# Mamba's chunk-end states: two sets of sums on four 32-column groups in place of a chain of six steps

## The chip, the cores and the metric

The kernel runs on one core of a Trainium2 chip. The metric is the device time of one execution in microseconds (us). TensorE is PE in the profile (its weight loads are PEld), VectorE is DVE, ScalarE is ACT, GpSimd is POOL, and SP is the engine that issues most DMAs.

## The reference

A decoder block: Mamba with two layers, cross-attention, and a mixture of experts, each behind a layer norm. Only Mamba matters here. Its recurrence, cut to the core:

```python
def scan_fn(carry, inp):
    h, v = carry
    dA_t, mi_t, C_t = inp
    v = BETA * v + mi_t          # BETA = 0.6
    h = dA_t * h + v
    y_t = jnp.einsum('ben,bn->be', h, C_t)
    return ((h, v), y_t)
```

`mi_t` is the outer product of a row of 512 channels (`delta * x`) and a row of 16 numbers (`B`). There are 4 sequences of 512 tokens and 2 layers. The inner recurrence `v` has a constant factor, so it is a convolution with powers of 0.6, and the kernel makes it with matmuls.

## The kernel before

Mamba is done in 8 **stages**, k = 0 to 7 (layer k // 4, sequence k % 4). A stage has 64 **pieces** i = 64k to 64k + 63; a piece is one of 16 states for 128 of the 512 channels, over all 512 tokens. For each pair of pieces TensorE makes `v` in two PSUM banks (`L631`, 24 matmuls), VectorE scans `h` over it (`L783`), GpSimd multiplies by `C` (`L987`), and TensorE adds the result of the piece 7 places back into an output bank by transposing it (`L610`, `pe_add_state`). ScalarE makes the decays `dA` (`L923`), issued 3 pieces ahead.

The matmul of `v` works on 6 chunks of 43 or 42 tokens for each half (256 tokens) of the sequence. `uT` holds a chunk in 64 partitions, rows 0 to 63 for the first half and 64 to 127 for the second. The first 16 rows of each block hold the state `v` at the end of the chunk before; the rest are the tokens. So before a stage can start, its chunk-end states must be known and put into these 16 rows. `bend` holds the weights that turn a block into its end state. That is what changes:

- `mid` (`L561`) adds up all 6 chunks of the first half, 12 matmuls of 64x256 (two groups of 64 columns), and gives the end state of the first half; ScalarE copies it (`act_carry`, `L802`).
- Then 5 steps, `c` and `ch` together (`L569`): the end of chunk c from the block of chunk c, in both halves at once, 4 matmuls of 64x256 on the four 64x64 tiles, then 4 copies of 16x256, and only then the next step.

Stage 0 has this chain in the open (`plan_first`). The front of a stage k + 1 is done during stage k: each engine's list `steps` says after which piece it does which part (`plan_front`); on TensorE the parts in `TILED` stand between the matmuls of `v` of a pair and the additions. There `mid` is at piece 50, and the five steps are at pieces 52, 54, 56, 58 and 60. I call the time from `mid` to the first `v` of the next stage the **end stretch**. `L550` (`u`) is the transposition of the chunks ahead of it.

Six PSUM banks are handed out by `banks_for`, in the order of `rows`: a single part takes the bank that was taken longest ago, a pair of pieces two neighbouring banks. `pe_open` waits until the bank's last user is through; for a pair's bank that is both scans of the pair.

Of the kernel before, what the change touches and what calls it, by code (L numbers as in the profile page):

```python
# [15 lines left out]
P = 128  # L16
BETA = 0.6
# [8 lines left out]
MID = 64  # L26
TILED = ("mid", "c", "ch")
# [48 lines left out]
def build(nc, d, out):  # L76
# [14 lines left out]
    with ExitStack() as ctx:  # L91
# [5 lines left out]
        def sb(c, name, shape, dt=F32):  # L97
            return c.enter_context(nc.sbuf_tensor(name, shape, dt))
# [102 lines left out]
        with ExitStack() as mc:  # L201
# [10 lines left out]
            ends = sb(mc, "ends", [P, NCH, 2])  # L212
# [15 lines left out]
            bend = lay(NCH * P).rearrange("p (c n) -> p c n", c=NCH)  # L228
# [47 lines left out]
            def plan_first():  # L276
# [23 lines left out]
                put("dve", "bcol")  # L300
                for m in range(ET):
                    put("pe", "d", m)
                    s += m % 2
                    put("act", "d", m)
# [25 lines left out]
                put("pe", "mid", 0)  # L330
                s += 1
                put("act", "mid", 0)
                for c in range(NCH - 1):
                    s += 1
                    for part in ("c", "ch"):
                        put("pe", part, c)
                    s += 1
                    for part in ("c", "ch"):
                        put("act", part, c)

            def plan_front(k, at, start):
# [16 lines left out]
                put(23, "dve", "bcol")  # L358
                for m in range(ET):
# [17 lines left out]
                put(50, "pe", "mid", 0)  # L377
                put(50, "act", "mid", 0)
                for c in range(NCH - 1):
                    for part in ("c", "ch"):  # L380
                        put(52 + 2 * c, "pe", part, c)
                        put(52 + 2 * c, "act", part, c)
# [89 lines left out]
            TAKER = {"xn": "dve", "p": "dve", "z": "act", "xp": "act", "dbcT": "dve", "d": "act", "u": "act", "mid": "act", "c": "act", "ch": "act", "bt": "dve", "bo": "dve", "ak": "dve", "aq": "dve", "ax": "act"}  # L472
# [27 lines left out]
            def pe_side(k, what, j=0):  # L500
# [54 lines left out]
                elif what == "mid":  # L555
                    bk = pe_open(k, "mid", 0)
                    pe.wait_ge(bend_done, k + 1)
                    pe.wait_ge(bank_act, emptied_by("act", k, "u", NCH - 1))
# [4 lines left out]
                elif what == "c":  # L563
                    sides = [pe_open(k, part, j) for part in ("c", "ch")]
                    pe.wait_ge(bank_act, emptied_by("act", k, "ch", j - 1) if j else emptied_by("act", k, "mid", 0))
                    for e0 in range(2):
                        for half in range(2):
                            r0 = half * KT
                            i = pe.matmul(sides[half][e0 * MT:(e0 + 1) * MT, e0 * HS:(e0 + 1) * HS], bend[r0:r0 + KT, j, 0:MT],  # L569
                                          uT[par][r0:r0 + KT, j, e0 * HS:(e0 + 1) * HS], start=True, stop=True, tile_position=(r0, e0 * MT))  # L570
                            if e0:
                                i.then_inc(bank_full, 1)
                    return
                elif what == "ch":
# [90 lines left out]
            def dve_side(k, what, j=0):  # L665
# [16 lines left out]
                elif what == "bcol":  # L682
                    dve.wait_ge(bank_full, filled(k, "dbcT", 0))
                    dve.wait_ge(ld_scan, 64)
                    if k >= 2:
# [4 lines left out]
                    dve.wait_ge(bank_dve, emptied_by("dve", k, "dbcT", 0))  # L690
                    dve.tensor_tensor(bend.rearrange("p c (g n) -> p c g n", g=2)[:, :, :, 0:NSTATE],
                                      bcol[:, par].unsqueeze(2).to_broadcast([P, NCH, 2, NSTATE]),
                                      ends[:].unsqueeze(3).to_broadcast([P, NCH, 2, NSTATE]), ALU.mult).then_inc(bend_done, 1)
# [105 lines left out]
            def act_carry(dst, bk):  # L799
                for e0 in range(2):  # L800
                    cols = slice(e0 * HS, (e0 + 1) * HS)
                    i = act.copy(dst[0:NSTATE, cols], bk[e0 * MT:e0 * MT + NSTATE, cols])  # L802
                i.then_inc(bank_act, 1)

            def act_side(k, what, j=0):
# [11 lines left out]
                elif what == "p":  # L817
                    bk = bank(k, "p", j)
                    act.wait_ge(bank_full, filled(k, "p", j))
                    if k == 0 and j == 0:  # L820
                        act.wait_ge(zeroed, 5)
                        act.wait_ge(ld_conv, 32)
# [64 lines left out]
                elif what in ("c", "ch"):  # L887
                    act.wait_ge(bank_full, filled(k, "ch", j))
                    act_carry(uT[par][KT * (what == "ch"):, j + 1, :], bank(k, what, j))
                elif what == "mid":  # L890
                    act.wait_ge(bank_full, filled(k, "mid", 0))
                    act_carry(uT[par][KT:, 0, :], bank(k, "mid", 0))
# [72 lines left out]
            def pool_mamba():  # L965
# [4 lines left out]
                pool.memset(bend, 0.0).then_inc(zeroed, 1)  # L970
                pool.wait_ge(zeroed, 5)
# [1030 lines left out]
def shape_constants():  # L2002
# [6 lines left out]
    ends = np.zeros((2, KT, len(CHUNKS), 2), np.float64)  # L2009
    for c, (t0, width) in enumerate(CHUNKS):  # L2010
        for half in range(2):
            ends[half, :, c, 0] = toep[half, :, width - 1]
        ends[0, NSTATE:NSTATE + width, c, 1] = BETA ** (CHUNKS[-1][0] + CHUNKS[-1][1] - 1 - t0 - np.arange(width))
    toep, ends = toep.reshape(P, QC), ends.reshape(P, len(CHUNKS), 2)
# [85 lines left out]
```

## Time and profile before

| | us |
|---|---|
| median of 3 runs (1557.35 to 1559.39) | 1558.73 |
| the profiled execution's own time | 1560.36 |
| its span | 1558.9 |
| Mamba until the first `v` of stage 0 | 78.4 |
| `mid` of stage 1 to `mid` of stage 7 (171.40 to 854.21), per stage | 113.8 |
| TensorE busy, share of the span | 88% |

All times are read on one execution's trace, from its first instruction. `x24` in a row is a count of instructions; an f32 matmul is recorded as two. "Idle before" in brackets names what the engine waited for.

### The profile page before, as it was taken

How to read it: one execution, taken by the hardware profiler on the slowest of the kernel's cores; microseconds unless marked ns; L12 is line 12 of the kernel's file. 1: busy time of each engine (PE TensorE's matmuls, PEld its weight loads, DVE VectorE, ACT ScalarE, POOL GpSimd, SP SyncE). 2: the span in 40 equal slices, each digit the busy share in tenths (PEclk: the TensorE clock that was granted, in tenths of full speed). 3: DMA queues.
4: the chain of work that ended last, by engine and by line, in shares of the span. 5: the costliest groups of instructions: out<-in, count | busy, mean ns of one | idle time of the engine just before them, and what ended most of it. 6: DMA issues, size and time to landing. Idle time of an engine off the chain costs nothing.

```text
span 1558.9 us, 46788 instructions
## 1 busy us (share of the span) xinstructions
PE 1372.9 (88%) x20442; PEld 975.9 (63%) x20442; DVE 1066.0 (68%) x1347; ACT 908.8 (58%) x1365; POOL 921.2 (59%) x802
## 2 busy tenths in 40 slices
PE   4679799999899899899899886878989887999997
PEld 2357577777677677667677775533444343499996
DVE  4189898798689688788788786577676771422223
ACT  3658567777767667767666765116555655434440
POOL 1159888989979969969969986530303000035541
PEclk8689999999999999999999998969999999999999
DMA  4102212222212212221221344370414100612225
GB/s 134 49 28 85 83 65 75 85 83 96 84 71 84 84 57 84 84 72 69 87 81 70 138 128 125 76 149 1 84 39 85 24 1 15 264 47 69 68 66 179
DMA packets 41497, 127.26 MB, mean 82 GB/s; under 512 B 8784, under 2 KB 21584, under 8 KB 32848
## 3 DMA queue, kind: packets, MB, share of 16 engines
q1 hardware_dynamic: 34736, 108.27, 21.4%
q0 software_dynamic: 6048, 14.95, 3.6%
q8 instruction: 163, 2.67, 0.7%
q10 hardware_dynamic: 512, 1.05, 0.4%
q14 instruction: 38, 0.31, 0.1%
HBM read 97.90 MB, written 9.57 MB: 69 GB/s over the span
## 4 chain that ended last, share of the span: by engine, by line
PE 59%; DVE 20%; issue 10%; ACT 4%; POOL 4%; DMA 2%; DVEq 0%; SPq 0%; ACTq 0%; POOLq 0%
PE psum L631 12%; DVE hst L783 9%; PE psum L610 8%; PE psum L1710 4%; PE psum L1722 4%; PE psum L1298 4%; PE psum L515 3%; POOL hst L987 3%; PE psum L601 3%; DVE overlay L679 2%; PE psum L1280 2%; DVE w_early L783 2%; PE psum L1652 2%; PE psum L1264 2%; DVE nmax L1419 2%
## 5 line engine op out<-in xcount | busy, mean ns | idle before, releaser
L987 POOL TENSOR_TENSOR hst<-hst,cb 128x512 f32<-128x512 f32 x399 | 513.5, 1306 | 125.7 <-DVE hst L783 110.3
L783 DVE TENSOR_TENSOR_SCAN hst<-dA,psum 128x512 f32<-128x512 f32 x399 | 467.1, 1204 | 140.7 <-PE psum L631 140.4
L610 PE MATMUL psum<-ident,hst 128*128 128x128 f32 x1596 | 236.5, 282 | 15.6 <-POOL hst L987 12.7
L610 PEld LDWEIGHTS psum<-ident,hst 128*128 128x128 f32 x1596 | 174.2, 141 | 66.3 <-issue 25.4
L923 ACT ACTIVATE dA<-delta,alog 128x512 f32<-128x512 f32 x256 | 177.0, 718 | 63.1 <-DVE hst L783 43.9
L923 ACT ACTIVATE dA<-xres,alog 128x512 f32<-128x512 f32 x256 | 176.1, 718 | 47.8 <-DVE hst L783 35.6
L1419 DVE TENSOR_REDUCE nmax<-psum 128x2 f32<-128x1024 f32 x128 | 154.6, 1220 | 55.3 <-PE psum L1264 54.8
L1348 ACT ACTIVATE pT<-psum 128x1024 f32<-128x1024 f32 x128 | 128.0, 1024 | 102.9 <-PE psum L1284 79.3
L631 PE MATMUL psum<-filt,c_early 64*64 64x86 f32 (+1 forms) x6144 | 147.2, 241 | 32.8 <-DVE hst L783 23.6
L631 PEld LDWEIGHTS psum<-filt,c_early 64*64 64x64 f32 x6144 | 126.6, 136 | 68.8 <-issue 39.9
L631 PE MATMUL psum<-filt,uT 64*64 64x86 f32 (+1 forms) x6144 | 144.8, 238 | 23.8 <-DVE hst L783 14.6
L631 PEld LDWEIGHTS psum<-filt,uT 64*64 64x64 f32 x6144 | 123.8, 133 | 57.2 <-issue 38.0
L987 POOL TENSOR_TENSOR w_early<-w_early,cb 128x512 f32<-128x512 f32 x113 | 144.5, 1290 | 24.5 <-DVE w_early L783 24.2
L783 DVE TENSOR_TENSOR_SCAN w_early<-dA,psum 128x512 f32<-128x512 f32 x113 | 133.8, 1204 | 30.2 <-PE psum L631 29.9
L1955 POOL DMA_INDIRECT overlay<-x_hat,origin x39 | 37.8, 970 | 186.6 <-DVE c_early L1901 175.1
L515 PE MATMUL psum<-overlay,w_early 128*128 128x512 f32 x256 | 124.4, 614 | 1.9 <-DVE hst L783 1.1
L1961 POOL DMA_INDIRECT y_choice<-yb,goal x39 | 38.5, 986 | 70.0 <-DVE yb L1915 70.0
L1800 ACT ACTIVATE ht<-psum 128x512 f32<-128x512 f32 x39 | 23.3, 597 | 93.9 <-PE psum L1710 93.9
L1710 PEld LDWEIGHTS psum<-xt,xn 128*128 128x128 f32 x624 | 75.6, 192 | 2.8 <-DVE xt L1907 0.9
L1710 PE MATMUL psum<-xt,xn 128*128 128x128 f32 x624 | 76.1, 275 | 0.7 <-DVE xt L1907 0.7
L679 DVE SCALAR_TENSOR_TENSOR overlay<-psum,w_cv,overlay 128x509 f32<-128x509 f32 (+2 forms) x96 | 71.1, 742 | 7.6 <-ACT overlay L823 5.3
L1722 PE MATMUL psum<-w_down,ht 128*128 x312 | 73.7, 380 | 0.0
(236 smaller groups left out, 2130.5 us busy)
## 6 DMA issues: line engine op xcount, KB each, us to landing
cb<-c_rows SPq DMA_DIRECT2D x64, 1024.0 KB, 4.7
qk_first<-w_early SPq DMA_DIRECT2D x64, 64.0 KB, 2.4
qk<-part SPq DMA_DIRECT2D x64, 64.0 KB, 2.7
w_up<-up_dram SPq DMA_DIRECT2D x8, 512.0 KB, 7.3
w_down<-down_dram SPq DMA_DIRECT2D x8, 512.0 KB, 12.9
w_up<-y_choice SPq DMA_DIRECT2D x8, 512.0 KB, 6.9
qk<-part POOLq DMA_DIRECT2D x48, 64.0 KB, 5.2
qk_first<-part SPq DMA_DIRECT2D x40, 64.0 KB, 2.4
```

The source lines that it names most:

```text
L515: i = pe.matmul(bk, w_in[:, kt, m8 * P:(m8 + 1) * P], xnT[:, kt, :], start=kt == 0, stop=kt == KD - 1)
L610: m = pe.matmul(psum[:, Y0 + et % EP, t * P:(t + 1) * P], hst(i)[:, t * P:(t + 1) * P], ident[:], start=n == 0 and t == 0, stop=n == NSTAT ...
L631: m = pe.matmul(halves_at[half][e0:e0 + MT, :, t0:t0 + width], uT[k % 2][r0:r0 + KT, c, et * P + e0:et * P + e0 + MT], filt[r0:r0 + KT, f ...
L679: i = dve.scalar_tensor_tensor(out=dst, in0=bk[:, 0:S - late], scalar=w_cv[:, l, j, tap:tap + 1], in1=dst, op0=ALU.mult, op1=ALU.add)
L783: dve.tensor_tensor_scan(hst(i), a, v, 0.0, ALU.mult, ALU.add).then_inc(scan_done, 1)
L923: act.activation(dA[:, a % NDA, :], delta[k % 2][:, et, :], ACT.Exp, scale=alog[:, k // B, et, n:n + 1]).then_inc(decay_done, 1)
L987: pool.tensor_tensor(h, h, cb[:, q % 2, state_of(i)[1] % GN, :], ALU.mult).then_inc(g_done, 1)
L1298: m = pe.matmul(psum[i * HROW:(i + 1) * HROW, PV, :], vt[:, cp, kv, c0:c0 + HROW], pT[:, (m0 + i // 2) % NPT, i % 2, :], start=kv == 0, st ...
L1348: act.activation(pT[:, m % NPT], pair(u, "score", s), ACT.Exp, scale=HDIM ** -0.5).then_inc(pair_act, 1)
L1419: dve.tensor_reduce(nmax[:, u % 2, t, 2 * j:2 * j + 2], pair(u, "max", r), AX.X, ALU.max, negate=True).then_inc(pair_dve, 1)
L1710: m = pe.matmul(psum[:, U0 + j % NUB, ft * P:(ft + 1) * P], wu[:, j % NWU, kt * F + ft * P:kt * F + (ft + 1) * P], xt[:, j % NXT, kt, :], ...
L1722: m = pe.matmul(out_bank(j)[:, 0:D], ht[:, j % NHT, ft, :], w_down[:, bass.ds(at + ft * D, D)], start=ft == 0, stop=ft == FT - 1)
```

## The change

The end states of a half are no longer a chain. `bend` becomes 6 x 6 blocks of 16 columns: for each end e and chunk c the powers of 0.6 that carry chunk c to end e. The ends of a half are six sums, over 1 to 6 chunks. `lo` makes the six ends of the first half, 21 matmuls of 16 x 512 with rows 0 to 63; each end has one of four 32-column groups in one of two banks (`LO_AT`), and the matmuls are issued in turns over the groups, 6 turns in all. ScalarE copies the six ends (16x512 each). `hi` makes five ends of the second half from rows 64 to 127, 15 matmuls in 5 turns (`HI_AT`), and 5 copies follow. `hi` needs the last end of `lo` and its copies. `bend` is now made by GpSimd (128x576) and no longer by VectorE (128x192, `L691`), in `plan_front` at piece 26.

```diff
-                put("pe", "mid", 0)
-                s += 1
-                put("act", "mid", 0)
-                for c in range(NCH - 1):
+                for part in ("lo", "hi"):
+                    for n in range(2):
+                        put("pe", part, n)
...
-                put(50, "pe", "mid", 0)
-                put(50, "act", "mid", 0)
-                for c in range(NCH - 1):
-                    for part in ("c", "ch"):
-                        put(52 + 2 * c, "pe", part, c)
-                        put(52 + 2 * c, "act", part, c)
+                for part, s in (("lo", 50), ("hi", 56)):
+                    for n in range(2):
+                        put(s, "pe", part, n)
+                        put(s + n, "act", part, n)
...
+LO_AT = ((5, 4, 3, 2), (None, None, 0, 1))
+HI_AT = ((4, 3, 2, 1), (None, None, 0, None))
...
-                    for c in range(NCH):
-                        for e0 in range(2):
-                            i = pe.matmul(bk[e0 * MT:(e0 + 1) * MT, e0 * HS:(e0 + 1) * HS], bend[0:KT, c, MID:MID + MT], uT[par][0:KT, c, e0 * HS:(e0 + 1) * HS],
-                                          start=c == 0, stop=c == NCH - 1, tile_position=(0, e0 * MT))
...
+                    sides = [pe_open(k, what, n) for n in range(2)]
+                    if what == "lo":
+                        pe.wait_ge(bend_done, k + 1)
+                        pe.wait_ge(bank_act, emptied_by("act", k, "u", NCH - 1))
+                    else:
+                        pe.wait_ge(bank_act, emptied_by("act", k, "lo", 1))
+                    at, r0 = (LO_AT, 0) if what == "lo" else (HI_AT, KT)
+                    queues = [[(n, at[n][g], c) for n in range(2) if at[n][g] is not None for c in range(at[n][g] + 1)] for g in range(4)]
+                    for turn in range(NCH):
+                        for g in range(4):
+                            if turn < len(queues[g]):
+                                n, end, c = queues[g][turn]
+                                i = pe.matmul(sides[n][g * BC:g * BC + NSTATE, :], bend[r0:r0 + KT, end, c, :], uT[par][r0:r0 + KT, c, :],
+                                              start=c == 0, stop=c == end, tile_position=(r0, g * BC))
+                    i.then_inc(bank_full, 2)
...
+                elif what in ("lo", "hi"):
+                    act.wait_ge(bank_full, filled(k, what, 1))
+                    for g, end in enumerate((LO_AT if what == "lo" else HI_AT)[j]):
+                        if end is not None:
+                            r0, c = (0 if what == "lo" else KT, end + 1) if end < NCH - 1 else (KT, 0)
+                            i = act.copy(uT[par][r0:r0 + NSTATE, c, :], bank(k, what, j)[g * BC:g * BC + NSTATE, :])
+                    i.then_inc(bank_act, 1)
...
+                if what == "bend":
+                    pool.wait_ge(bank_dve, emptied_by("dve", k, "dbcT", 0))
...
+                    pool.tensor_tensor(bend, bcol[:, par].unsqueeze(1).to_broadcast([P, NCH, NCH, NSTATE]),
+                                       ends[:].unsqueeze(3).to_broadcast([P, NCH, NCH, NSTATE]), ALU.mult).then_inc(bend_done, 1)
```

TensorE's order in the end stretch of stages 1 to 7 (here during stage 3) was, from the pair at piece 50 on (`L631` is `v`, `L610` the additions, `L561` is `mid`, `L569` is `c` with `ch`):

```order
L561 MATMUL psum<-c_early,overlay 64x256 x12
L610 MATMUL psum<-ident,hst 128x128 x8
L631 MATMUL psum<-filt,uT 64x2x43 x16
L631 MATMUL psum<-filt,uT 64x2x42 x8
L569 MATMUL psum<-c_early,overlay 64x256 x4
L610 MATMUL psum<-ident,hst 128x128 x8
```

The last four rows come five times. In the changed kernel the lines are numbered `L568` (`lo`, `hi`), `L627` (`v`) and `L606` (additions), and at the same place stands:

```order
L568 MATMUL psum<-c_early,overlay 16x512 x21
L606 MATMUL psum<-ident,hst 128x128 x8
L627 MATMUL psum<-filt,uT 64x2x43 x16
L627 MATMUL psum<-filt,uT 64x2x42 x8
L606 MATMUL psum<-ident,hst 128x128 x8
L627 MATMUL psum<-filt,uT 64x2x43 x16
L627 MATMUL psum<-filt,uT 64x2x42 x8
L606 MATMUL psum<-ident,hst 128x128 x8
L627 MATMUL psum<-filt,uT 64x2x43 x16
L627 MATMUL psum<-filt,uT 64x2x42 x8
L568 MATMUL psum<-c_early,overlay 16x512 x15
```

Six small insertions have become two large ones, at pieces 50 and 56; pieces 58, 60 and 62 follow with nothing between. The banks follow: before, pieces 54, 56, 58, 60 and 62 (from stage 2's pieces on) all get the two banks that the pair just ahead of them left; after, every pair from 52 to 62 gets banks of a user at least three entries of `rows` back.

ScalarE's order there was (`L923` decays, `L802` copies of ends), the last two rows five times:

```order
L923 ACTIVATE dA<-xres,alog 128x512
L802 COPY uT<-psum 16x256 x2
L923 ACTIVATE dA<-xres,alog 128x512 x2
L802 COPY uT<-psum 16x256 x4
L923 ACTIVATE dA<-xres,alog 128x512 x2
```

and is now (`L910` decays, `L878` copies):

```order
L910 ACTIVATE dA<-xres,alog 128x512
L878 COPY uT<-psum 16x512 x4
L910 ACTIVATE dA<-xres,alog 128x512
L878 COPY uT<-psum 16x512 x2
L910 ACTIVATE dA<-xres,alog 128x512 x5
L878 COPY uT<-psum 16x512 x4
L910 ACTIVATE dA<-xres,alog 128x512
L878 COPY uT<-psum 16x512
```

There are 11 copies in four places instead of 22 in six.

## Rows read from the trace of the kernel before

**Rows 1.** The page, busy time and share of the span, instructions.

```profile
PE 1372.9 (88%) x20442; PEld 975.9 (63%) x20442; DVE 1066.0 (68%) x1347; ACT 908.8 (58%) x1365; POOL 921.2 (59%) x802
```

**Rows 2.** Waits of VectorE in the end stretches 171:202, 290:310, 627:652.

```profile
DVE hst L783 <- PE psum L631: 4.5, 2, 2.3
...
DVE hst L783 <- PE psum L631: 2.9, 5, 1.4
DVE w_early L783 <- PE psum L631: 2.8, 2, 2.3
...
DVE hst L783 <- PE psum L631: 8.8, 6, 2.3
DVE w_early L783 <- PE psum L631: 1.4, 1, 1.4
```

**Rows 3.** Timeline of stage 0's chain: start, us, engine, line.

```profile
58.09 5.21 PE L561 MATMUL psum<-c_early,overlay 64*64 64x256 f32 x24 [1.30 <-ACT c_early L885]
65.43 1.50 ACT L802 COPY c_early<-psum 16x256 f32<-16x256 f32 x4 [1.36 <-PE psum L569]
...
78.40 3.69 PE L631 MATMUL psum<-filt,c_early 64*64 64x86 f32 x96 [1.63 <-ACT c_early L802]
```

**Rows 4.** Windows (PE, PEld, DVE, ACT, POOL busy; granted clock; DMA share; GB/s).

```profile
59.00:63.30 4.30, 4.30 (x21) 2.42 (x17) 0.00 (x0) 0.00 (x0) 0.00 (x0) 0.50 0.00 0
...
78.90:82.10 3.20, 3.20 (x92) 2.94 (x84) 1.57 (x2) 3.19 (x5) 0.20 (x1) 0.50 0.00 0
83.00:89.00 6.00, 4.01 (x151) 3.62 (x152) 5.86 (x15) 5.69 (x8) 4.00 (x5) 1.00 0.01 3
```

**Rows 5.** Timeline, attention: matmuls on four 32-column groups.

```profile
1104.48 1.07 PE L1298 MATMUL psum<-pT,vt 128*32 128x512 f32 x8
...
1107.76 1.92 PE L1298 MATMUL psum<-pT,vt 128*32 128x512 f32 x16
```

**Rows 6.** Timeline, ScalarE: four copies of 512 columns from PSUM.

```profile
47.15 2.03 ACT L827 COPY xres<-psum 128x512 f32<-128x512 f32 x4
```

**Rows 7.** Timeline of stage 6's end stretch, during stage 5.

```profile
627.09 2.76 PE L561 MATMUL psum<-uT,overlay 64*64 64x256 f32 x24
...
629.78 1.09 PE L610 MATMUL psum<-ident,hst 128*128 128x128 f32 x8
...
649.40 1.12 PE L631 MATMUL psum<-filt,c_early 64*64 64x86 f32 x48 [1.14 <-DVE hst L783]
...
650.63 4.55 DVE L783 TENSOR_TENSOR_SCAN hst<-dA,psum 128x512 f32<-128x512 f32 x4 [1.38 <-PE psum L631]
```

**Rows 8.** Timeline around stage 2's end stretch, during stage 1.

```profile
290.21 2.76 PE L561 MATMUL psum<-c_early,overlay 64*64 64x256 f32 x24
...
309.25 6.77 DVE L783 TENSOR_TENSOR_SCAN hst<-dA,psum 128x512 f32<-128x512 f32 x6 [0.20 <-PE psum L631]
```

**Rows 9.** Timeline, TensorE: `v` of stages 1 and 5, `mid` of stage 3.

```profile
201.75 0.46 PE L631 MATMUL psum<-filt,uT 64*64 64x86 f32 x12
...
398.92 0.38 PE L561 MATMUL psum<-uT,overlay 64*64 64x256 f32 x1
...
537.50 1.12 PE L631 MATMUL psum<-filt,c_early 64*64 64x86 f32 x48
...
539.57 1.12 PE L631 MATMUL psum<-filt,c_early 64*64 64x86 f32 x48
```

**Rows 10.** Timeline of stage 1's end stretch, during stage 0.

```profile
171.40 2.81 PE L561 MATMUL psum<-uT,overlay 64*64 64x256 f32 x24 [0.43 <-DVE hst L783]
...
174.32 4.08 DVE L756 TENSOR_SCALAR stat<-stat 128x8 f32<-128x8 f32 x1
```

**Rows 11.** By line: `bend` on VectorE, and GpSimd's filters; timeline of GpSimd.

```profile
L691 DVE TENSOR_TENSOR overlay<-bcol,ends x8: 357/1441/1446, 36.8 to 810.5; 128x192 f32<-128x192 f32 x8
...
L959 POOL TENSOR_TENSOR filt<-toep,bcol x64: 1049/1054/1507, 51.0 to 877.8; 128x516 f32<-128x516 f32 x64
...
586.38 2.70 POOL L987 TENSOR_TENSOR hst<-hst,cb 128x512 f32<-128x512 f32 x2 [1.67 <-DVE hst L783]
```

More of the change, by code:

```diff
@@ L25 @@
 MT = 64
-MID = 64
-TILED = ("mid", "c", "ch")
+LO_AT = ((5, 4, 3, 2), (None, None, 0, 1))
+HI_AT = ((4, 3, 2, 1), (None, None, 0, None))
+TILED = ("lo", "hi")
 EP, NFILT = 2, 9
@@ L211, in build @@
             toep = sb(mc, "toep", [P, QC])
-            ends = sb(mc, "ends", [P, NCH, 2])
+            ends = sb(mc, "ends", [P, NCH, NCH])
             keep = sb(mc, "keep", [P, 1])
@@ L227, in build @@
             bcol = sb(mc, "bcol", [P, 2, NCH, NSTATE])
-            bend = lay(NCH * P).rearrange("p (c n) -> p c n", c=NCH)
+            bend = lay(NCH * P)[:, 0:NCH * NCH * NSTATE].rearrange("p (e c n) -> p e c n", e=NCH, c=NCH)
             filt = sb(mc, "filt", [P, NFILT, NCH, 2, QC])
@@ L300, in plan_first @@
                 put("dve", "bcol")
+                put("pool", "bend")
                 for m in range(ET):
@@ L358, in plan_front @@
                 put(23, "dve", "bcol")
+                put(26, "pool", "bend")
                 for m in range(ET):
@@ L376, in plan_front @@
                     put(45 + c // 2 * 2, "act", "u", c)
-                put(50, "pe", "mid", 0)
-                put(50, "act", "mid", 0)
-                for c in range(NCH - 1):
-                    for part in ("c", "ch"):
-                        put(52 + 2 * c, "pe", part, c)
-                        put(52 + 2 * c, "act", part, c)
+                for part, s in (("lo", 50), ("hi", 56)):
+                    for n in range(2):
+                        put(s, "pe", part, n)
+                        put(s + n, "act", part, n)
             def plan_back(k, at, s):
@@ L554, in pe_side @@
                     return
[L555 to L558, printed above, removed]
-                    for c in range(NCH):
-                        for e0 in range(2):
-                            i = pe.matmul(bk[e0 * MT:(e0 + 1) * MT, e0 * HS:(e0 + 1) * HS], bend[0:KT, c, MID:MID + MT], uT[par][0:KT, c, e0 * HS:(e0 + 1) * HS],
-                                          start=c == 0, stop=c == NCH - 1, tile_position=(0, e0 * MT))
[L563 to L574, printed above, removed]
@@ L689, in dve_side @@
                                              op0=ALU.mult, op1=ALU.add).then_inc(bank_dve, 1)
[L690 to L693, printed above, removed]
                 elif what == "clip":
@@ L797, in act_silu_z @@
                 act.activation(sz[k % 2], sz[k % 2], ACT.Silu).then_inc(sz_done, 1)
[L799 to L803, printed above, removed]
             def act_side(k, what, j=0):
@@ L820, in act_side @@
                     if k == 0 and j == 0:
-                        act.wait_ge(zeroed, 5)
+                        act.wait_ge(zeroed, 4)
                         act.wait_ge(ld_conv, 32)
@@ L886, in act_side @@
                              bank(k, "u", j).rearrange("p (c e x) -> p c e x", c=2, e=ET)).then_inc(bank_act, 1)
[L887 to L892, printed above, removed]
+                elif what in ("lo", "hi"):
+                    act.wait_ge(bank_full, filled(k, what, 1))
[4 more added lines that the diff above has]
+                    i.then_inc(bank_act, 1)
                 elif what == "x_roots":
@@ L969, in pool_mamba @@
                 pool.memset(dbc[:], 0.0).then_inc(zeroed, 1)
-                pool.memset(bend, 0.0).then_inc(zeroed, 1)
-                pool.wait_ge(zeroed, 5)
+                pool.wait_ge(zeroed, 4)
                 for x in at_steps("pool", "first"):
@@ L2008, in shape_constants @@
         toep[:, NSTATE + s, s:] = BETA ** np.arange(QC - s)
[L2009 to L2014, printed above, removed]
+    ends = np.zeros((2, KT, len(CHUNKS), len(CHUNKS)), np.float64)
+    for e, (last, wide) in enumerate(CHUNKS):
+        ends[:, :NSTATE, e, 0] = BETA ** (last + wide)
+        for c, (t0, width) in enumerate(CHUNKS[:e + 1]):
+            ends[:, NSTATE:NSTATE + width, e, c] = BETA ** (last + wide - 1 - t0 - np.arange(width))
+    toep, ends = toep.reshape(P, QC), ends.reshape(P, len(CHUNKS), len(CHUNKS))
     keep = (np.arange(P) % KT >= NSTATE).astype(f)[:, None]
```

16 lines of the change are left out of this document (10 added, 6 removed).

## The prediction

> **What bounds the kernel now.** The page comes first: TensorE is busy for 88% of the span, the others for 58 to 68% [rows 1]. But an average over stages says little, so I go to the places that the change touches: stage 0's chain, which has nothing beside it, and the seven end stretches, which lie between other work.
>
> Stage 0's chain is read on the timeline. `mid` starts at 58.09, the first `v` at 78.40 [rows 3]. These 20.3 us are all on the path: 5.2 of `mid`, then five times a step of TensorE and 1.5 us of copies. The reader should also see the clock: while `mid` ran without a gap it was granted 0.50, that is 1.2 GHz, and it came up only after `v` had run densely on all four 64x64 tiles at 78.9 to 82.1 [rows 4].
>
> For the end stretches I read VectorE's waits, since its scans are what the next stage begins with. In stage 6's stretch VectorE waits 10.2 us for `v`, in stage 2's 5.7, in stage 1's 4.5 [rows 2]. The 10.2 come from the banks: the pair's `v` itself waits 1.14 us for the scans of the pair ahead, VectorE then 1.38 for `v` [rows 7]. In stage 2's stretch the banks fall otherwise and TensorE runs through. Measured from `mid` to the scan of piece 62, it takes 23.54 us in stage 6 (627.09 to 650.63) and 19.04 in stage 2 (290.21 to 309.25) [rows 7, 8]. Is such a difference kept? From `mid` of stage 2 to `mid` of stage 3 there are 108.7 us [rows 8, 9], against 113.8 for the mean stage. So yes, almost one to one: what scans gain in an end stretch the whole gains.
>
> **Stage 0.** How fast four 32-column groups run is shown in attention: 4 matmuls of 512 columns take 1.07 us, 8 take 1.92 [rows 5], so four more cost 0.85 us at full clock. One alone at two groups and 256 columns costs (2.69 for 12, below) 0.22 us, so 0.43 for a pair of groups, 0.85 for 512 columns: the four groups run side by side at no loss. A turn of `lo` or `hi` is therefore 0.85 us at 2.4 GHz. At 1.2 GHz I scale from `mid`: 5.21 us for 6 turns of 256 columns [rows 3], so 10.4 for the 6 turns of `lo` and 8.7 for the 5 of `hi`. Copies: four of 512 columns take 2.03 us [rows 6], 0.51 each, so 3.0 for six and 2.5 for five. They replace 22 copies at 0.375 [rows 3], 8.2 us, with 5.5. With three handovers at 0.1 us the chain ends at 58.1 + 10.4 + 3.0 + 8.7 + 2.5 + 0.4 = 83.1: **4.7 us later**. TensorE does 36 matmuls of 512 columns where it did 32 of 256, and that costs more than the 11 copies and ten handovers saved. Bounds: +3.9 if 16 rows copy faster than 128, +6 if slower or if the next `v` stays at 0.50 for longer.
>
> **The end stretch of stages 3 to 7.** At 1.00, `mid` holds TensorE from 627.09 to 629.78, 2.69 us for 6 turns of 0.43, so 0.13 of it is drain [rows 7]. Then `lo` is 6 x 0.853 + 0.13 = 5.25 and `hi` 4.40. A pair with its additions takes 2.07 us (537.50 to 539.57 [rows 9]), 1.05 of it `v`. From the start of `lo`: additions at 5.25, `v` of piece 52 at 6.27, 54 at 8.34, 56 at 10.41, `hi` 11.35 to 15.75, `v` of 58 at 16.77, 60 at 18.84, 62 at 20.9. No bank holds this up: each pair's bank was left two pairs back. VectorE's first scan follows its `v` by 1.23 (649.40 to 650.63 [rows 7]) and two take 2.33, so 58 is scanned from 18.0, 60 from 20.35, 62 from 22.7. Before, that was 23.54: **0.85 gained, five times: -4.25**. VectorE still waits, once about 5 us for `lo` and once 3.5 for `hi`, where it waited many times. Queued behind `lo` on TensorE are the additions and the next `v`, and GpSimd, which is behind by several pieces there, has work meanwhile. Bounds: 0 to -1.4 each, where TensorE's own first `v` of the next stage arrives (23.0 against 24.4).
>
> **Stage 2.** Its stretch had no such bank waits, so there the longer matmuls count in full: 22.7 against 19.04, **+3.65** (bounds +2.5 and +3.9).
>
> **Stage 1.** Here VectorE itself is held by one instruction of 4.08 us at 174.32, which covers all of `lo` [rows 10]. Its 4.5 us of waits for `v` [rows 2] came from pairs that got the bank of the pair ahead; they do not any more. I take **-4**, bounds 0 and -4.8.
>
> **The rest of a stage.** The new order of banks is the same in every stage from 1 on, and is that which stage 1 had: from its first `v` to the next `mid` it took 88.46 us (201.75 to 290.21), stage 4 took 89.59 from 537.50 to 627.09 [rows 7, 8, 9]. If the banks are the reason, four stages gain 1.1 each. Bounds 0 and -4.5; I take half, **-2.3**.
>
> **`bend`** leaves VectorE (1.44 us, with the next `v` not there yet) and goes to GpSimd. The nearest row is the filter, 516 columns in 1.05 us, so 1.2 for 576; ahead of the scans that follow GpSimd idles 1.67 [rows 11], which hides it. Without that cover it would be 1.2 x 7 = 8 us. In stage 0 GpSimd has nothing to do yet. ScalarE is blocked while `lo` runs, as its copy stands there; the decays it issues 3 ahead just suffice. Both: 0.
>
> **Sum**: +4.7 - 4 + 3.65 - 4.25 - 2.3 = -2.2. The profiled execution took 1560.4 by its own time, 1.6 above the median of the runs, so I apply the difference to the median: 1558.7 - 2.2 = **1556.5**. All bounds together give -9 to +10 in theory; hardly all at one end, so 1549 to 1563 for this case. A measurement of this kernel tells 0.2%, 3.1 us, from nothing: below 1555.6 is faster, above 1561.8 slower. Chance of this case 0.62.
>
> **Rival 1, slower: the clock falls in `lo`.** `lo` and `hi` use half of the rows and 16 of each 32 columns, for 5.25 and 4.40 us without a break. `mid` used half of the rows, and at 0.50 did not bring the clock up in 4.3 us of unbroken work [rows 4]. Light work for that long at 1.00 is nowhere in this trace: `mid` lasts 2.7. If the clock falls during `lo` and `hi`, they and the pairs behind them run at half. Each microsecond of TensorE's work done at 0.50 costs one more. With a third of the 9.65 us of `lo` and `hi` at half, 3.2 us are lost per end stretch, 23 over seven: 1580 (1567 to 1605, for one sixth to two thirds). It decides from the point at which more than 0.3 us per stretch is done at half. For it speaks the row of `mid`, against it that the seven `mid` stretches leave the clock alone. Chance 0.20.
>
> **Rival 2: the clock rises in stage 0.** `lo` runs 10 us unbroken, and work might bring the clock up. Then `lo` saves half of its extra 5.2, `hi` 4.3: 6.9 less, 1549.6. Against it stands `mid`, 4.3 us at 0.50. Chance 0.06. The Trainium skill, TensorE: Matmul & The Clock Gate, section on the HAM clock gate, says that idling throttles the clock and sustained matmul activity releases it, with no word on how much of the array is used. By that rule Rival 2 would be what happens, and Rival 1 could not; `mid` in this trace disagrees with it.
>
> **Rival 3, slower: two lumps starve VectorE and nothing is gained elsewhere.** Stage 1 gives 0, stages 3 to 7 give 0, the rest 0, and 4.7 + 3.65 stay: 1567. GpSimd, with `bend` added, could do that if it can't keep up. Against it: over the span it is busy 59% [rows 1], if more than that inside Mamba, and its pieces stay behind by less than the 7 that TensorE allows. Chance 0.08.
>
> **Rival 4: 64-row tiles don't run four abreast.** The row that shows four groups has 128 rows. With two abreast `lo` takes 21 x 0.853 / 2 = 9.0 and `hi` 6.4, 5.8 us more per stretch and 12 in stage 0: 1609. Chance 0.04.
>
> **How the numbers follow.** Below 1548 lies little. To 1584 the range takes in the case itself, Rivals 2 and 3 and the nearer half of Rival 1. Faster: 0.4 of the likeliest case and Rival 2, 0.31. Same: half of the likeliest and a little of Rival 3, 0.34. Slower: 0.35.
>
> **What would show it.** The first `v` of stage 0 at 83.1 and its clock at 0.50 throughout; one block of `lo` of 5.3 us and of `hi` of 4.5 in each end stretch, at 1.00; from `lo` to the scan of piece 62 22.7 in all of stages 2 to 7, and a stage of 112 us; no wait of `v` for the scan of the pair ahead. Wrong would be: a clock of 0.50 inside an end stretch, `lo` above 6 us at full clock, or GpSimd without idle time in the first half of a stage.

## The result and the profile after

| | before | after |
|---|---|---|
| median of 9 runs each, same chip (us) | 1559.63 (1556.42 to 1561.96) | 1566.21 (1562.29 to 1573.4) |
| ratio, 95% interval | | 1.0049 (1.0031 to 1.0068) |

The change makes the kernel 0.5% slower. The forecast was 1556.5, 2.2 us faster. The profiled execution of after is its fastest run (1562.29), so its trace shows less of the loss than the median has. Of the runs below one took 2585 us, the profiled one of the kernel with own chunks and `bend` at 23, so that kernel's ratio is of its other five runs and no trace of it is read.

The page after has TensorE at 1410.5 us where it was at 1372.9 [rows 1], 38 more. In the seven end stretches `lo` and `hi` (5.32 and 4.46, below) stand for `mid` (2.76 [rows 7]) and five steps of about 0.65 each: 7 x 3.7 = 26 of the 38. Stage 0 has 3 more; the rest I did not follow up.

```profile
PE 1410.5 (90%) x20506; PEld 975.7 (63%) x20506; DVE 1065.2 (68%) x1339; ACT 894.4 (57%) x1277; POOL 930.4 (60%) x809
```

The timeline of stage 0's chain, which answers to [rows 3]:

```profile
57.70 5.31 PE L568 MATMUL psum<-c_early,overlay 64*16 64x512 f32 x42 [1.30 <-ACT c_early L871]
63.05 3.53 ACT L878 COPY c_early<-psum 16x512 f32<-16x512 f32 x6 [5.49 <-PE psum L568]
...
66.73 8.69 PE L568 MATMUL psum<-c_early,overlay 64*16 64x512 f32 x30 [3.71 <-ACT c_early L878]
75.45 2.94 ACT L878 COPY c_early<-psum 16x512 f32<-16x512 f32 x5 [8.87 <-PE psum L568]
...
78.44 4.39 PE L627 MATMUL psum<-filt,c_early 64*64 64x86 f32 x144 [3.02 <-ACT c_early L878]
```

`lo` took 5.31 us and not 10.4: the clock was at 1.00 here. `hi` took the 8.7 forecast, at 0.50. The first `v` comes at 78.44, as before. In two of the three executions traced below that have this stage 0 unchanged, `lo` takes 8.0 and 8.4 us and the first scan comes 4.4 and 5.5 us later than here; of that more below.

Next the end stretch that answers to [rows 7]. (There and in the prediction it is called that of stage 6; counted from 0, as everywhere else, it is that of stage 5, and lies in stage 4; the `v` at 537.50 in [rows 9] is likewise that of stage 4.) Timelines of TensorE and of VectorE:

```profile
628.88 5.32 PE L568 MATMUL psum<-uT,overlay 64*16 64x512 f32 x42
...
640.35 4.46 PE L568 MATMUL psum<-uT,overlay 64*16 64x512 f32 x30
```
```profile
628.99 2.33 DVE L775 TENSOR_TENSOR_SCAN hst<-dA,psum 128x512 f32<-128x512 f32 x2 [1.43 <-PE psum L627]
636.42 5.67 DVE L775 TENSOR_TENSOR_SCAN hst<-dA,psum 128x512 f32<-128x512 f32 x5 [5.10 <-PE psum L627]
...
647.03 1.22 DVE L775 TENSOR_TENSOR_SCAN w_early<-dA,psum 128x512 f32<-128x512 f32 x1 [3.84 <-PE psum L627]
```

`lo` 5.32, `hi` 4.46, two waits of VectorE of 5.1 and 3.8: the end stretch is as it was worked out. So I read where every scan of a stage begins in both traces (512 scans each), and took differences:

| scans of a stage (us) | stage 0 | 1 | 2 | 3 | 4 | 5 | 6 |
|---|---|---|---|---|---|---|---|
| piece 50 to 62, before | 28.39 | 18.72 | 23.23 | 23.22 | 23.22 | 23.22 | 23.23 |
| piece 50 to 62, after | 24.54 | 22.40 | 22.48 | 22.41 | 22.51 | 22.41 | 23.41 |
| piece 28 to 29, before | 1.45 | 1.45 | 1.45 | 1.45 | 1.45 | 1.45 | 1.45 |
| piece 28 to 29, after | 2.56 | 2.55 | 2.54 | 2.55 | 2.55 | 2.55 | 2.55 |

(The end stretch of stage k + 1 lies in stage k.) The third and fourth line are the discovery: each of stages 0 to 6 loses 1.1 us at one place, 7.7 us in all. The timelines of VectorE and of GpSimd there, in stage 4:

```profile
592.49 0.40 DVE L689 TENSOR_SCALAR xraw<-delta 128x512 f32<-128x512 f32 x1
...
593.94 1.50 DVE L689 TENSOR_SCALAR xraw<-delta 128x512 f32<-128x512 f32 x1
595.36 1.21 DVE L775 TENSOR_TENSOR_SCAN hst<-dA,psum 128x512 f32<-128x512 f32 x1
```
```profile
592.54 1.37 POOL L934 TENSOR_TENSOR overlay<-bcol,ends 128x576 f32<-128x576 f32 x1
593.88 4.04 POOL L981 TENSOR_TENSOR hst<-hst,cb 128x512 f32<-128x512 f32 x3
```

The **clip** (the `TENSOR_SCALAR` of `L689`, four in a stage) takes 0.40 us once and 1.50 the next time. The long one began 0.06 us after the first of the three products had begun, and ended 0.3 us behind the end of that product (595.16). The clip before it began 0.05 us ahead of `bend`: it took 0.40, and `bend` 1.37 where it takes 1.16 to 1.18 in stage 0 and in the runs that have it at 23 or 31. `bend` (`L934`) stands just ahead of this product and moved it there. `bend` thus has a price, though nobody waits for its result.

### The profile page after: what moved, and what is told of

Same layout as the page of the kernel before. It is cut to its first block, busy times and chain, and to the rows that moved or that the text cites. A ratio compares the mean times of both kernels' runs of the same rounds, so it can differ in the third digit from the quotient of the medians.

```text
span 1560.8 us, 46811 instructions
## 1 busy us (share of the span) xinstructions
PE 1410.5 (90%) x20506; PEld 975.7 (63%) x20506; DVE 1065.2 (68%) x1339; ACT 894.4 (57%) x1277; POOL 930.4 (60%) x809
## 4 chain that ended last, share of the span: by engine, by line
PE 53%; DVE 25%; issue 10%; POOL 6%; ACT 4%; DMA 2%; DVEq 0%; SPq 0%; ACTq 0%; POOLq 0%
DVE hst L775 11%; PE psum L627 8%; PE psum L606 6%; PE psum L568 4%; POOL hst L981 4%; PE psum L1704 4%; PE psum L1292 4%; PE psum L1716 4%; DVE w_early L775 3%; DVE overlay L675 3%; PE psum L1274 2%; PE psum L513 2%; PE psum L597 2%; PE psum L1646 2%; PE psum L1258 2%
## 5 line engine op out<-in xcount | busy, mean ns | idle before, releaser
L606 PE MATMUL psum<-ident,hst 128*128 128x128 f32 x1596 | 240.3, 285 | 11.8 <-POOL hst L981 8.7
L910 ACT ACTIVATE dA<-delta,alog 128x512 f32<-128x512 f32 x256 | 177.5, 719 | 71.9 <-DVE hst L775 50.9
L606 PEld LDWEIGHTS psum<-ident,hst 128*128 128x128 f32 x1596 | 177.6, 143 | 60.8 <-issue 19.6
L910 ACT ACTIVATE dA<-xres,alog 128x512 f32<-128x512 f32 x256 | 176.1, 718 | 52.8 <-DVE hst L775 40.1
L627 PE MATMUL psum<-filt,c_early 64*64 64x86 f32 (+1 forms) x6144 | 146.3, 240 | 24.6 <-DVE hst L775 11.9
L627 PEld LDWEIGHTS psum<-filt,c_early 64*64 64x64 f32 x6144 | 125.3, 135 | 61.1 <-issue 50.5
L627 PE MATMUL psum<-filt,uT 64*64 64x86 f32 (+1 forms) x6144 | 145.9, 240 | 13.3 <-DVE hst L775 5.4
L627 PEld LDWEIGHTS psum<-filt,uT 64*64 64x64 f32 x6144 | 124.7, 135 | 46.3 <-issue 39.8
```

Of the source, the lines that this page charges most:

```text
L606: m = pe.matmul(psum[:, Y0 + et % EP, t * P:(t + 1) * P], hst(i)[:, t * P:(t + 1) * P], ident[:], start=n == 0 and t == 0, stop=n == NSTAT ...
L627: m = pe.matmul(halves_at[half][e0:e0 + MT, :, t0:t0 + width], uT[k % 2][r0:r0 + KT, c, et * P + e0:et * P + e0 + MT], filt[r0:r0 + KT, f ...
L910: act.activation(dA[:, a % NDA, :], delta[k % 2][:, et, :], ACT.Exp, scale=alog[:, k // B, et, n:n + 1]).then_inc(decay_done, 1)
```

## The experiments

Ratios are to runs of the kernel before on the same chip, taken at the same time; the changed kernel's is 1.0049, and 0.001 is 1.56 us. Intervals are 95%. The difference of two such ratios is uncertain by 4 to 6 us.

**Where does `bend` cost?** First it is moved behind the clips.

```diff
-                put(26, "pool", "bend")
+                put(31, "pool", "bend")
```

> The changed kernel with GpSimd's bend moved from piece 26 to piece 31, nothing else. In the changed kernel every stage from 0 to 6 loses 1.1 us between the scans of pieces 28 and 29: there VectorE's fourth clip takes 1.50 us where it took 0.40, and it begins 0.06 us after a product of GpSimd has begun. Theory A (the clip is held until GpSimd's product ends, and bend moved GpSimd's products into its way): with bend behind the clips the step from scan 28 to 29 is 1.45 us again in each of seven stages, 7 x 1.1 = 7.9 us less than the changed kernel: 1558.3. Theory B (GpSimd's 1.4 us more of work per stage hold VectorE back wherever they stand): no gain, 1566. In between if the later maxima of VectorE, pieces 35 to 38, are caught in the same way: 1562.

1.0058 (1.0037 to 1.0080): no gain, Theory A's sum fails. Yet its mechanism shows: 28 to 29 is 1.45 us again in all seven stages. The microsecond is lost later. From piece 36 to 37 the scans are 1.0 us late (2.70 us in stage 4, after 1.71), but by piece 40 that is made good. From 45 to 46 they fall back by 1.1 us (2.50, after 1.40), and that stays. Timelines of GpSimd, of VectorE and of TensorE:

```profile
603.58 1.17 POOL L934 TENSOR_TENSOR overlay<-bcol,ends 128x576 f32<-128x576 f32 x1
...
608.64 4.66 POOL L981 TENSOR_TENSOR hst<-hst,cb 128x512 f32<-128x512 f32 x3
```
```profile
608.81 1.64 DVE L699 TENSOR_TENSOR delta<-delta,xraw 128x512 f32<-128x512 f32 x1
...
611.51 0.66 DVE L699 TENSOR_TENSOR delta<-delta,xraw 128x512 f32<-128x512 f32 x1
```
```profile
623.21 1.16 PE L548 MATMUL psum<-ident,overlay 64*64 64x64 f32 x64 [1.03 <-POOL overlay L939]
```

A maximum (`max`) is held at 608.81, 1.64 in place of 0.66; that is the step from 36 to 37. The loss that stays is TensorE's: the transpositions of the next stage's chunks (`L548`) wait 1.03 us for GpSimd, at this place in all seven stages, and the next `v` stands behind them. From piece 26 to 46 GpSimd works without an idle moment (in after from 588.4 to past 624), so its 1.2 to 1.4 us more of work there push everything behind. Theory B is right in that stretch. Is it right everywhere? So `bend` goes to VectorE, or on GpSimd ahead of that stretch:

```diff
+                        dve.tensor_tensor(bend, bcol[:, par].unsqueeze(1).to_broadcast([P, NCH, NCH, NSTATE]),
+                                          ends[:].unsqueeze(3).to_broadcast([P, NCH, NCH, NSTATE]), ALU.mult).then_inc(bend_done, 1)
```

> The changed kernel with bend of stages 1 to 7 made by VectorE right behind bcol, where before made its own. VectorE had 1.44 us of it there before with no wait for v, and waits 1.56 us for v in the changed kernel. Its 576 columns should take 0.8 us by itself (128x256 take 0.40) and up to 1.4 more if it is held by a product of GpSimd: it costs 0 to 0.6 us per stage. Theory A (the products of GpSimd, moved by 1.4 us, catch the clip): the step from scan 28 to 29 is 1.45 again, 1566.2 - 7.9 + 2 = 1560 (1558 to 1562). Rival (bend costs the same wherever it stands): 1566.

1.0010 (0.9989 to 1.0030), the time that Theory A gave, and 6 us less than after. The timeline of VectorE, piece 23:

```profile
581.09 1.83 DVE L688 TENSOR_TENSOR overlay<-bcol,ends 128x576 f32<-128x576 f32 x1
```

It takes 1.83 us, with a product of GpSimd beside it, but most of that lies in a wait for `v` that was there anyway: the scan of piece 24 comes 0.2 us later, and that of piece 26 on time.

```diff
-                put(26, "pool", "bend")
+                put(23, "pool", "bend")
```

> The changed kernel with GpSimd's bend moved from piece 26 to piece 23, nothing else. At piece 26 it stands behind the products of 24, 25 and 26, in a stretch in which GpSimd has no idle time until piece 46; behind the product of 23 GpSimd waits 1.97 us for the next scan, and bend with 1.2 to 1.4 us fits into that. Theory A (bend costs what GpSimd has no idle time for): the 1.1 us per stage come back in stages 0 to 6, 28 to 29 is 1.45 us and no later step grows: 1566.2 - 7.9 = 1558.3, between 1557 and 1560. Theory B (GpSimd's bend costs wherever it stands, as at piece 31, where the clips were free and the time came back at pieces 36 and 45): 1566 to 1568.

1.0013 (0.9998 to 1.0027), 0.0036 or 5.6 us less than after (plus or minus 3.7). The timelines of GpSimd and VectorE:

```profile
588.76 1.16 POOL L934 TENSOR_TENSOR overlay<-bcol,ends 128x576 f32<-128x576 f32 x1
590.47 2.70 POOL L981 TENSOR_TENSOR hst<-hst,cb 128x512 f32<-128x512 f32 x2 [0.55 <-DVE hst L775]
```
```profile
596.27 0.40 DVE L689 TENSOR_SCALAR xraw<-delta 128x512 f32<-128x512 f32 x1
```

The same instruction on the same engine, three pieces earlier, lies in GpSimd's idle time (0.55 us are left of it), and the clip is 0.40. 28 to 29 is 1.45 in all seven stages, and at piece 46 four of the seven stages stand 1.1 us ahead of after, the other three 0.5 to 0.7; behind that, pieces 46 to 50 differ between executions, so that pieces 0 to 50 of stages 0 to 6 together are only 2.9 us shorter in this trace. Theory A holds in the form: it costs what GpSimd has no idle time for. Theory B is refuted as "wherever it stands".

**Stage 0.** The old chain there alone (`OLD = (0,)`; the engines' code of before for `mid`, `c` and `ch` is kept beside the new, and VectorE makes the old `bend` of stage 0):

```diff
+                if 0 in OLD:
+                    put("pe", "mid", 0)
+                    s += 1
+                    put("act", "mid", 0)
+                    for c in range(NCH - 1):
...
+                        for part in ("c", "ch"):
+                            put("pe", part, c)
```

> The changed kernel with the chain of before in stage 0 and lo and hi in stages 1 to 7. The banks fall as in the changed kernel but for two pieces of stage 1. In the profiled execution of the changed kernel the first v of stage 0 comes at 80.5 as lo ran at 1.00; with lo at 0.50 it would come at 83.1; before it came at 78.4. Theory A (stage 0 costs 2.1 to 4.7 us): 1566.2 - 3.5 = 1562.7, between 1561.5 and 1564, and the runs lie within 3 us of each other, not within 11 as those of the changed kernel, if the clock of lo in stage 0 is what varies. Rival (stage 0's cost is made up in stage 0 itself, where VectorE waits elsewhere): 1566.

1.0015 (1.0000 to 1.0030): 0.0034 or 5.3 us less than after (plus or minus 3.7). The runs lie within 6.6 us, not 3 as expected, against 11 of after. (The text above names 80.5 as after's first `v`; that is the first scan, `v` came at 78.4, and at 1.00 `lo` cost nothing.) Is it the clock? The run with `bend` at 31 has the same stage 0 and by chance a late clock. Windows of its `lo` (two) and `hi`:

```profile
59.40:61.90 2.50, 2.48 (x24) 0.77 (x28) 0.00 (x0) 0.00 (x0) 0.00 (x0) 0.99 0.00 0
61.90:67.50 5.60, 5.51 (x22) 0.94 (x14) 0.00 (x0) 0.05 (x1) 0.00 (x0) 0.50 0.00 0
71.00:79.80 8.80, 8.67 (x30) 1.57 (x30) 0.00 (x0) 0.00 (x0) 0.00 (x0) 0.50 0.01 2
```

The same windows of after:

```profile
57.70:63.00 5.30, 5.29 (x42) 1.33 (x42) 0.00 (x0) 0.00 (x0) 0.00 (x0) 1.00 0.00 0
66.70:75.40 8.70, 8.67 (x30) 1.56 (x30) 0.00 (x0) 0.00 (x0) 0.00 (x0) 0.50 0.01 2
```

In the first the clock fell to 0.50 after 2.5 us of `lo`, with TensorE at work without a break. In all four traces with this stage 0 `hi` was at 0.50 throughout; `lo` took 5.3 twice and 8.0 and 8.4 once each. Then matmuls that nobody reads fill the gaps of stage 0:

```diff
+            def keep_busy(n):
+                for _ in range(n):
+                    pe.matmul(psum[:, Y0, 0:P], ident[:], ident[:], start=True, stop=True)
...
+                    if k == 0:
+                        keep_busy(5 if what == "lo" else 12)
```

> The changed kernel with 27 matmuls of 128x128 in stage 0 that nobody reads (5 ahead of lo, 12 between lo and hi while ScalarE copies, 10 ahead of the first v). The clock of TensorE in stage 0 was 1.00 or fell to 0.50 in the middle of lo, and was 0.50 in all of hi. Theory A (idle time and half-filled work bring the clock down, and it is worth 4.3 us in hi and up to 5 in lo): the clock is at 1.00 in hi and in the first v; hi takes 4.4 us, the first v comes at 76 to 79 and not at 78.4 to 82.8, the time is 1561 to 1563 and the runs lie closer. Theory B (the half-filled matmuls themselves bring it down): lo and hi still fall to 0.50, the extra matmuls delay hi by up to 2.5 us: 1567 to 1570.

0.9997 (0.9982 to 1.0013): 0.0052 or 8 us less than after. Windows of `lo` and `hi`:

```profile
59.70:65.00 5.30, 5.30 (x44) 1.22 (x42) 0.00 (x0) 0.00 (x0) 0.00 (x0) 1.00 0.01 3
68.60:73.10 4.50, 4.37 (x30) 0.96 (x30) 0.00 (x0) 0.08 (x1) 0.00 (x0) 1.00 0.00 0
```

Both at 1.00, `hi` in 4.46, the first `v` at 76.22. Theory A, and the fillers cost nothing that shows. They do two things at once, fill idle time and use the whole array, and which of the two keeps the clock up was not tried apart. The runs still lie 8.7 us apart, so the clock of stage 0 explains the cost but not all of the spread.

**What made the end stretch of before long?** The kernel before, with one line changed:

```diff
-        elif who == "scan":
+        elif who == "scan" or name[1] == "c":
```

> The kernel before with one line changed: c and ch of a step take two neighbouring banks, as a pair of pieces does, so that pieces 54 to 62 no longer get the banks of the pair ahead. The chain of six steps stays. Theory A (the banks, not the chain, made the end stretches long): scans 50 to 62 take 18.7 us in all stages as in stage 1, where they took 23.2 in five: 5 x 4.5 = 22.5 us less than before, 1537. Theory B (the chain of steps holds the end stretch): 1559 to 1560. Half of it if GpSimd or ScalarE cannot follow: 1548.

0.9912 (0.9886 to 0.9938), 13.7 us faster than before. Timelines of TensorE and VectorE, the stretch of stage 5:

```profile
625.81 2.76 PE L561 MATMUL psum<-uT,overlay 64*64 64x256 f32 x24
```
```profile
630.79 2.33 DVE L783 TENSOR_TENSOR_SCAN hst<-dA,psum 128x512 f32<-128x512 f32 x2 [2.32 <-PE psum L631]
634.51 2.33 DVE L783 TENSOR_TENSOR_SCAN hst<-dA,psum 128x512 f32<-128x512 f32 x2 [1.38 <-PE psum L631]
...
642.35 2.33 DVE L783 TENSOR_TENSOR_SCAN hst<-dA,psum 128x512 f32<-128x512 f32 x2 [0.20 <-PE psum L631]
645.20 4.55 DVE L783 TENSOR_TENSOR_SCAN hst<-dA,psum 128x512 f32<-128x512 f32 x4 [0.51 <-PE psum L631]
```

Piece 62 is scanned at 645.20, 19.06 us after piece 50 (626.14); before it was 23.22. The old chain with six steps needs 3.4 us less than the two lumps. Of the 22.5 expected, 20.7 appear in the five stretches; 4.8 go again in stage 1, where TensorE stands still for 2.1 us in the middle of the additions ahead of `mid`, with a mean clock of 0.94 and 0.89 in the 10 us before and behind 290, and 3.2 in stage 7, which differs between all executions. Theory A on the mechanism; two fifths of its sum are lost elsewhere.

**Is it TensorE's work that holds after's end stretch?** Each end from its own chunk alone:

```diff
-                    queues = [[(n, at[n][g], c) for n in range(2) if at[n][g] is not None for c in range(at[n][g] + 1)] for g in range(4)]
+                    queues = [[(n, at[n][g], c) for n in range(2) if at[n][g] is not None for c in (at[n][g],)] for g in range(4)]
...
-                                              start=c == 0, stop=c == end, tile_position=(r0, g * BC))
+                                              start=True, stop=True, tile_position=(r0, g * BC))
```

> The changed kernel with 11 matmuls in place of 36: each end is made from its own chunk alone, and the products that carry earlier chunks and the start state through one or more whole chunks are left out (their factor is at most 0.6 to the power 42, 5e-10). lo and hi then take two turns each, 1.7 us, and not 5.25 and 4.40. Theory A (TensorE holds the end stretch, and its longer matmuls are what the change costs): scans 50 to 62 take 22.4 - 6.2 = 16.2 us if TensorE alone holds them, not below 17 as pairs take 2.07 and 2.3 on VectorE; I take 18: 4.4 less in seven stages, 31, and stage 0 gets its first v 10 us earlier (1.7 or 3.4 of lo in place of 5.3 to 10.4, 3.4 of hi in place of 8.7): 1566 - 31 - 9 = 1526, between 1518 and 1535. Theory B (waits for the copies and bank order hold it, as the six copies and five copies stay): no more than 2 us per stage and 5 in stage 0: 1547.

0.9846 (0.9824 to 0.9868), 1535.9. Timelines of TensorE and VectorE, the same place:

```profile
608.50 1.91 PE L568 MATMUL psum<-uT,overlay 64*16 64x512 f32 x12
...
616.56 1.90 PE L568 MATMUL psum<-uT,overlay 64*16 64x512 f32 x10
```
```profile
608.65 2.33 DVE L775 TENSOR_TENSOR_SCAN hst<-dA,psum 128x512 f32<-128x512 f32 x2 [1.38 <-PE psum L627]
612.63 5.67 DVE L775 TENSOR_TENSOR_SCAN hst<-dA,psum 128x512 f32<-128x512 f32 x5 [1.64 <-PE psum L627]
...
620.68 1.22 DVE L775 TENSOR_TENSOR_SCAN w_early<-dA,psum 128x512 f32<-128x512 f32 x1 [1.28 <-PE psum L627]
```

TensorE has 6.0 us less to do in a stretch, and in stages 1 to 6 pieces 50 to 62 fall from 22.4 to 16.7, by 5.7. Nothing else was changed, copies and banks stand as they were: TensorE holds these stretches, Theory B is refuted. The total fell short of 1526 for three reasons that the trace shows. Pieces 0 to 50 take 0.9 us more (89.3 for 88.4, mean of stages 1 to 6): the step from scan 1 to 2 of stages 2 to 7, for one, is 2.3 us and not 1.1. GpSimd used to catch up in the waits of the end stretch and has less of them now; that this is the reason was not tried. In stage 0 the stretch did not shrink but grew, from 24.54 to 26.75, with the clock twice at 0.50 in it. And stage 7 took 7.4 us more, of which the cause is open.

**Do the repairs add up?** Four combinations of these edits. In the last, the fillers stand ahead of `mid`, of each step and of the first `v`.

> Both edits: each end from its own chunk alone (the products through whole chunks are left out), and bend of GpSimd behind the product of piece 23. If the two costs are independent, the time is that of the run with the own chunk alone less 7.9: about 1518. If the shorter end stretch lets GpSimd fall behind, so that it holds the stage, the second edit gives more or less than that by over 3 us.

0.9793 (0.9772 to 0.9815), 1529.3: 8.3 us less than own chunk alone (plus or minus 4.8), which agrees with the 7.9 expected for independent costs. With stage 0 kept busy too:

> Ends from their own chunk alone (products through whole chunks left out), bend behind piece 23, and stage 0 kept busy. Own chunk and bend at 23 gave 0.9793. In stage 0 lo and hi are two turns each, so the clock is worth no more than 1.7 us in each, and the first v comes at 3 us less with 27 extra matmuls that may not fit into the gaps: 0.9775 if they fit, 0.980 if they don't.

0.9765 (0.9734 to 0.9795), 1527.3, the fastest kernel of this study, which leaves out the products named above. Its lead over the 0.9793, 0.0028, is within the noise. `lo` and `hi` of stage 0 took 1.9 us each at 1.00, and the first `v` came at 67.7, 2.1 earlier than with own chunks alone.

> The changed kernel with both repairs that leave its sums as they are: bend behind the product of piece 23, and stage 0 kept busy. By themselves they gave 0.0036 and 0.0052 of the ratio of 1.0049. If they add up: 0.996, some 6 us under before: what the forecast's terms without its two errors give, and still far from the 0.991 of the old chain with better banks, since lo and hi hold TensorE 4.8 us longer than mid and five steps. If one hides the other: 0.998 to 1.000.

0.9953 (0.9936 to 0.9971), 1556.0: additive, and below before.

> The kernel before with neighbouring banks for c and ch (0.9912 of before by itself) and, in stage 0 alone, matmuls of 128x128 that nobody reads (5 ahead of mid, 3 or 4 ahead of each of the five steps, 4 ahead of the first v). Theory (the clock costs the same in the old chain): mid takes 2.7 us and not 5.2, each of the five steps 0.4 us less, the first v comes about 4.5 us earlier than 78.4 to 79.7: the ratio is 0.9912 - 0.0029 = 0.988. Rival (the copies hold the chain and the extra matmuls get in the way): 0.991 to 0.993.

0.9884 (0.9854 to 0.9913), 1545.2; the ratio alone does not tell it from the 0.9912 without fillers, the trace does. Timeline of TensorE in stage 0:

```profile
57.85 2.81 PE L563 MATMUL psum<-c_early,overlay 64*64 64x256 f32 x24
...
61.48 0.66 PE L573 MATMUL psum<-c_early,overlay 64*64 64x256 f32 x8
...
73.01 2.90 PE L640 MATMUL psum<-filt,c_early 64*64 64x86 f32 x144 [0.56 <-ACT c_early L811]
```

`mid` takes 2.8 and not 5.2 us, the first `v` comes at 73.0 and not at 78.4 to 79.6. This is the fastest kernel that makes all the products of before.

## Why the prediction was wrong

The step that failed is **`bend`: 0**. I wrote that GpSimd's idle 1.67 us "ahead of the scans that follow" hide it, "which hides it. Without that cover it would be 1.2 x 7 = 8 us". The cover is real, but it lies ahead of piece 24's product, and the planner's entry at piece 26 puts `bend` behind it, as the first of a stretch with no idle time. It cost 1.1 us a stage, 7.7 us by the trace, 5.6 (plus or minus 3.7) by the ratio of the run that moved it into the cover. With +7.7 the sum of -2.2 is +5.5 us; +6.6 was measured. With `bend` moved into the cover the ratio was 1.0013, not to be told from 1, where the forecast was 0.9986. So `bend` is the larger part of the miss and not all of it: 4 us (plus or minus 2) remain that the terms below do not place.

- **Stage 0, +4.7**: in agreement with the ratio (5.3 when undone, plus or minus 3.7), but not shown to be right. I had `lo` at 0.50 for certain; the clock differs from run to run. The four traces with this stage 0 have the first scan at 79.6, 80.6, 85.0 and 86.0, the three with the old one at 80.5, 81.7 and 81.7: 1.5 us later on average, and never `lo` at 10.4.
- **Stages 3 to 7, -0.85 each**: right in four of them (pieces 50 to 62 of stages 2 to 5: -0.75, -0.81, -0.71, -0.82), +0.18 in the fifth.
- **Stage 2, +3.65**: +3.68.
- **Stage 1, -4**: -3.85 by the scans of stage 0. The number is right, the reason only in part. I gave its waits to the banks and wrote under Rival 1 that "the seven `mid` stretches leave the clock alone". Here they did not: before, the clock was at 0.50 twice in this stretch, behind waits of 3.81 and 2.80 us in which TensorE stood still, and a `v` then took 1.98 us where it takes 1.12. The window, and timelines of TensorE and VectorE before:

```profile
181.20:184.60 3.40, 3.25 (x62) 2.64 (x60) 1.15 (x2) 3.30 (x6) 3.40 (x4) 0.50 0.01 2
```
```profile
180.09 0.66 PE L569 MATMUL psum<-uT,overlay 64*64 64x256 f32 x8 [3.81 <-DVE hst L783]
...
182.35 1.98 PE L631 MATMUL psum<-filt,c_early 64*64 64x86 f32 x48 [0.15 <-DVE w_early L783]
```
```profile
184.46 2.33 DVE L783 TENSOR_TENSOR_SCAN hst<-dA,psum 128x512 f32<-128x512 f32 x2 [2.25 <-PE psum L631]
```

  At full clock each of the two waits of 2.3 would have been 0.86 shorter: by this estimate about 1.7 of the 3.85 are the clock's. After the change no wait of TensorE in this stretch is longer than 1.8 us, and the clock stays at 1.00 in this trace.
- **The rest, -2.3**: pieces 0 to 50 of stages 1 to 6 changed by +1.8; less `bend`'s 6.6 that is -4.9, right in sign and just outside its bound of -4.5. Stage 0's lose 2.2, half of it `bend`. That the order of banks is the reason no run shows.
- **Rival 1** (clock falls in the end stretches): `lo` 5.3 and `hi` 4.46 in all seven are full speed; it does not occur. What I feared for 1.00 under light work does happen, but in stage 0, where the work around is light too.
- **Rival 2**: the clock can be at 1.00 in `lo`, though not because `lo` raised it. By the Trainium skill (TensorE: Matmul & The Clock Gate, The HAM clock gate) idling throttles and sustained activity releases. Stage 0 with `bend` at 31 disagrees: the clock fell in the middle of 8 us of unbroken work on half of the rows and 16 of each 32 columns, and did not rise in 8.7 us of `hi`, which is the same kind of work.
- **Rival 3**: its time, 1567, is near by luck, for another reason; the end stretches did gain.
- **Rival 4**: 5.3 us for 21 matmuls is four abreast; it does not occur.

That a clip is held by GpSimd was visible before: `bend` on VectorE had taken 1.44 us for 192 columns and 0.36 once [rows 11]. I took 1.44 for its duration. The Trainium skill, SBUF — State Buffer, section SBUF: two separate sides, says that VectorE (in a two-port mode, or with two inputs in SBUF) and GpSimd share a pair of ports, and that the one which starts second is blocked for the whole instruction of the other. The trace agrees: 1.50 and 0.40 for one clip, 1.64 and 0.66 for one maximum, while scans, which take one of their inputs from PSUM, take 1.2 everywhere. The instruction of 4.08 us in [rows 10] has the same sign. GpSimd works beside it without a break until 178.38, and it ends at 178.41; in each of the 12 traces that are read here it takes 4.1 to 5.9 us and ends 0.03 to 0.04 us after GpSimd first falls idle. So the wait can last through several instructions of GpSimd; that it is the ports that hold it was not tried.

What stays open: the spread of the runs beyond stage 0 (6.6 us with the old chain there, and 12.4 for the 26 runs of before in the first set of experiments, so much of it is no matter of the change), and why stage 7 differs by up to 8 us between executions (100.8 to 109.2 from its first scan to its last, over all kernels).

## What to carry to other kernels

Work moved to "an engine with idle time" is free only where it stands in the queue: look at the idle time directly ahead of that place, not at the share. Before restructuring a stage that waits, ask which resource it waits for; here one line about banks was worth 14 us where the new algorithm lost 7. A share of that 7 was `bend`'s place alone: with it and stage 0 repaired the new algorithm is 7 us faster than before, half of what the one line gives. When an edit adds matmul time to a stretch that TensorE holds, count it in full and take the gain from buffers apart from it, as they can be had separately.

## What the runs showed of the hardware

- Four 32-column groups with 64-row operands run side by side: 21 matmuls of 512 f32 columns in 5.3 us at 1.00, 6 turns of 0.85 and the drain.
- Copying 16 rows of 512 from PSUM takes ScalarE 0.58 us, no less than 128 rows at 0.51 [rows 6].
- Matmuls of 128x128 whose result nobody reads, put into waits of 0.9 to 3.7 us, kept the clock at 1.00 through work on part of the array that otherwise got 0.50, and halved its time (`hi` 8.69 to 4.46, `mid` 5.21 to 2.81).
- A VectorE instruction of 0.40 us on SBUF can take 1.50 beside GpSimd. Beginning 0.06 us behind a product it took 1.50; beginning 0.05 us ahead of `bend` it took 0.40, and `bend` 1.37 for 1.16.
- TensorE's clock fell to 0.50 behind waits of 3.81 and 2.80 us in the end stretch that lies in stage 0, and a `v` took 1.98 for 1.12.
